# The high and low q row of a node side by side in the table, one window load per edge group: a graph network layer on one NeuronCore

## What is computed

```python
h  = maximum(layernorm(x), 0)
eq = h @ Wq + bq          # per node
ek = h @ Wk + bk          # per node
e  = edge_attr @ We + be  # per edge
m  = relu(eq[dst] + ek[src] + e)
ft = segment_sum(m, dst)
out = x + (ft @ Wr + br)
```

## Time and profile before

| | |
|---|---|
| median of 3 runs | 1135.48 us (1135.22 to 1139.48) |
| the profiled execution, device time | 1134.75 us |
| its span in the profile | 1132.9 us |
| mean granted clock of TensorE | 0.995 of full speed |
| PE, DVE, ACT, POOL busy | 96%, 83%, 76%, 75% of the span |
| HBM traffic | 272 GB/s over the span |

### The profile page before, as it was taken

The page is one execution under the profiler, slowest core; times in us unless marked ns, Lnnn a source line. Parts: engine busy times, 40 slices in busy tenths (PEclk is TensorE's granted clock), DMA queues, the critical chain, the costliest instruction groups (busy, mean ns, idle before and its releaser), DMA issues.

```text
span 1132.9 us, 28337 instructions
## 1 busy us (share of the span) xinstructions
PE 1091.0 (96%) x9166; PEld 1065.9 (94%) x9166; DVE 945.5 (83%) x1382; ACT 857.9 (76%) x1373; POOL 849.3 (75%) x949
## 2 busy tenths in 40 slices
PE   9979999999999999999999999999999999999998
PEld 8978999999999999999999999999999999998997
DVE  7778888888888888888888888888888888888887
ACT  7957877777777777787777777777777777777774
POOL 7877777777777777777777777777777777777773
PEclk9998999999999999999999999999999999999999
DMA  9789898999989988899998998889998899988882
GB/s 301 225 258 286 271 287 280 282 276 286 285 273 288 280 276 281 274 285 282 282 282 273 286 287 274 281 275 286 283 280 281 280 283 279 288 275 256 268 252 87
DMA packets 171122, 309.10 MB, mean 273 GB/s; under 512 B 30817, under 2 KB 117358, under 8 KB 171038
## 3 DMA queue, kind: packets, MB, share of 16 engines
q1 hardware_dynamic: 130590, 198.79, 53.3%
q0 software_dynamic: 39888, 108.97, 34.4%
q10 hardware_dynamic: 560, 0.52, 0.1%
HBM read 281.20 MB, written 26.95 MB: 272 GB/s over the span
## 4 chain that ended last, share of the span: by engine, by line
POOL 68%; issue 23%; PE 3%; DMA 2%; DVE 1%; ACT 1%; SPq 1%; POOLq 0%; ACTq 0%; DVEq 0%
POOL k_rows L727 67%; PE p_sum L1339 1%; PE p_edge L1339 1%; DMA hn<-in_x 1%; DMA k_table<-k_rows 0%; PE p_turn L1359 0%; DMA ft<-in_x 0%; POOL hn L651 0%; DVE stats L1008 0%; DVE p_edge L1182 0%; PE p_sum L1443 0%; SPq L489 0%; ACT k_rows L797 0%; POOL edge L665 0%; SPq L478 0%
## 5 line engine op out<-in xcount | busy, mean ns | idle before, releaser
L727 POOL DMA_INDIRECT k_rows<-k_table,src_idx x796 | 765.3, 961 | 246.3 <-issue 241.9
L1339 PE MATMUL p_edge<-we_hi,edge_hi 128*128 128x256 f32 x1662 | 473.7, 285 | 28.1 <-DVE m_lo L1191 22.3
L1339 PE MATMUL p_edge<-we_hi,edge_lo 128*128 128x256 f32 x1662 | 462.5, 278 | 0.0
L1339 PE MATMUL p_edge<-we_lo,edge_hi 128*128 128x256 f32 x1662 | 461.2, 277 | 0.0
L1182 DVE TENSOR_TENSOR p_edge<-p_edge,k_rows 128x1024 f32<-128x1024 f32 x208 | 256.0, 1231 | 162.4 <-DMA k_rows<-k_table,src_idx 133.8
L878 ACT ACTIVATE m_hi<-p_edge 128x1024 fp32r<-128x1024 f32 x208 | 213.8, 1028 | 205.3 <-DVE p_edge L1182 205.3
L1339 PEld LDWEIGHTS p_edge<-we_hi,edge_hi 128*128 128x128 f32 x1662 | 314.9, 189 | 48.9 <-issue 23.0
L1339 PEld LDWEIGHTS p_edge<-we_lo,edge_hi 128*128 128x128 f32 x1662 | 315.8, 190 | 0.0
L1339 PEld LDWEIGHTS p_edge<-we_hi,edge_lo 128*128 128x128 f32 x1662 | 313.5, 189 | 0.0
L1157 DVE TENSOR_TENSOR edge_lo<-edge,edge_hi 128x1024 fp32r<-128x1024 f32 x208 | 253.2, 1217 | 2.9 <-ACT edge_hi L822 2.9
L1191 DVE SCALAR_TENSOR_TENSOR m_lo<-p_edge,m_hi 128x1024 fp32r<-128x1024 f32 x208 | 252.6, 1215 | 0.5 <-ACT m_hi L878 0.5
(11 more groups left out here) (154 smaller groups left out, 1104.7 us busy)
## 6 DMA issues: line engine op xcount, KB each, us to landing
edge<-in_edges SPq DMA_DIRECT2D x208, 512.0 KB, 5.2
rel_row<-rel_table SPq DMA_DIRECT2D x208, 96.0 KB
q_win<-q_table SPq DMA_DIRECT2D x416, 48.0 KB
k_rows<-k_table,src_idx POOLq DMA_INDIRECT x796
q_table<-hn SPq DMA_DIRECT2D x46, 256.0 KB
pre<-in_x SPq DMA_DIRECT2D x55, 128.0 KB, 5.6
out_rows<-pre SPq DMA_DIRECT2D x55, 128.0 KB, 1.7
k_table<-k_rows SPq DMA_DIRECT2D x23, 256.0 KB, 4.8
```

Source lines behind the costliest of these rows:

```text
L727: nc.gpsimd.indirect_dma_start(out=k_rows[:, slot, j, :], out_offset=None, in_=k_table, in_offset=bass.IndirectOffsetOnAxis(ap=offsets, ax ...
L1339: ins = nc.tensor.matmul(target, a(h), b[:, h, :], start=(start and h == 0 and n == 0), stop=(stop and h == HALVES - 1 and n == 2))
```

## The change

A node's high and low q row lie side by side in `q_table`: row 2v is the high row of node v, row 2v + 1 its low row. A window of 48 nodes is then 96 rows in one piece, and `load_window` is one transfer of 96 rows in place of two of 48. Partition p of `q_win` now holds the row of node p // 2 of the window, so `lane_node` is computed anew: the parity of the partition number, halved, is taken from half the iota. This adds one integer instruction on DVE (`bitwise_and`) and one wait ahead of `lane_wrap`; `lane_node` takes a scalar_tensor_tensor in place of a tensor_tensor. Stores of q rows write 2 KB in one piece per partition where they wrote two of 1 KB. PE waits for 16 a group in place of 32.

```diff
-    q_table = nc.dram_tensor("q_table", (2, NODE_BLOCKS * LANES, D), F32R, kind="Internal").ap()
+    q_table = nc.dram_tensor("q_table", (2 * NODE_BLOCKS * LANES, D), F32R, kind="Internal").ap()
...
-    q_blocks = q_table.rearrange("s (b p) d -> s b p d", p=LANES)
+    q_blocks = q_table.rearrange("(b p s) d -> b p s d", p=LANES, s=2)
...
-        lane_id = sb("lane_id", [2 * WIN, 1], F32)
+        lane_id = sb("lane_id", [2 * WIN, 1], I32)
...
-        PREP_STEPS = SPAN_STEPS + 4 + CHUNKS + 2
+        PREP_STEPS = SPAN_STEPS + 5 + CHUNKS + 2
...
-                    sp.dma_start(q_blocks[:, b].rearrange("s p d -> p s d").bitcast(F32),
+                    sp.dma_start(q_blocks[b].bitcast(F32),
                                  q_parts[:, b].bitcast(F32)).then_inc(s_qfirst[v], 16)
...
                 after(sp, s_prod, n - 4)
-                for s in range(2):
-                    sp.dma_start(q_win[s * WIN:(s + 1) * WIN, slot, :].bitcast(F32),
-                                 q_table[s, bass.ds(w0, WIN), :].bitcast(F32)).then_inc(s_win[slot], 16)
+                sp.dma_start(q_win[0:2 * WIN, slot, :].bitcast(F32),
+                             q_table[bass.ds(w0 * 2, 2 * WIN), :].bitcast(F32)).then_inc(s_win[slot], 16)
...
-                if isinstance(it, int):
-                    target = q_blocks[:, it + FIRST_Q].rearrange("s p d -> p s d")
-                else:
-                    target = q_blocks[:, bass.ds(it + FIRST_Q, 1)].rearrange("s a p d -> (a p) s d")
+                target = q_blocks[it + FIRST_Q]
...
-            nc.gpsimd.iota(lane_raw[:], pattern=[[WIN, PASSES]], base=0, channel_multiplier=1,
+            nc.gpsimd.iota(lane_raw[:], pattern=[[2 * WIN, PASSES]], base=0, channel_multiplier=1,
...
+                nc.vector.tensor_scalar(lane_id[:], lane_id[:], 1, None, ALU.bitwise_and).then_inc(s_prep, 1)
...
-                nc.vector.tensor_scalar(lane_wrap[:], lane_id[:], float(WIN), float(WIN), ALU.is_ge, ALU.mult)\
-                    .then_inc(s_prep, 1)
+                dve.wait_ge(s_prep, SPAN_STEPS + 1)
+                nc.vector.tensor_scalar(lane_wrap[:], lane_id[:], 0.5, None, ALU.mult).then_inc(s_prep, 1)
...
-                dve.wait_ge(s_prep, SPAN_STEPS + 5)
+                dve.wait_ge(s_prep, SPAN_STEPS + 6)
...
-                nc.vector.tensor_tensor(lane_node[:], lane_raw[:], lane_wrap[:].to_broadcast([2 * WIN, PASSES]),
-                                        ALU.subtract).then_inc(s_prep, 1)
+                nc.vector.scalar_tensor_tensor(lane_node[:], lane_raw[:], 0.5, lane_wrap[:].to_broadcast([2 * WIN, PASSES]),
+                                               ALU.mult, ALU.subtract).then_inc(s_prep, 1)
...
-                pe.wait_ge(s_win[slot], 32 * (body + 1))
+                pe.wait_ge(s_win[slot], 16 * (body + 1))
```

## The result

| | before | after |
|---|---|---|
| median of 14 runs | 1134.72 us | 1141.18 us |
| lowest, highest | 1132.40, 1139.48 | 1139.34, 1146.09 |
| ratio, 95% interval | | 1.0058 (1.0047 to 1.0069) |
| span of the profiled execution | 1132.9 us | 1139.4 us |

The forecast was 1134.7 us, the range ended at 1138.0.

The account below looks back on a forecast made before the run. POOL was taken to bound the kernel, at 1.25 us a gather. The start's -0.8 us and DVE's +0.05 us made about -0.8 us against the median of 1135.48, so 1134.7 us; range 1131.0 to 1138.0.

Parts of the forecast that it names:

- What bounds the kernel: Whole loop: POOL's gathers set the pace, 0.947 + 0.30 = 1.25 us each, 1034 us of the 1132.9 us span.
- One q transfer for two, the loop: SP's window loads in the loop: 208 issues fewer, nothing waits on them; 0 taken, 0 to -1 us kept.
- becomes longer waiting at L489: SP's queue in the loop: about 0.5 us a group freed only lengthens SP's wait for PE to free the slot.
- The prediction's own sign of being wrong: Loop: among its signs, the 3.5 us of stretched gathers becoming 6 or more would show the prediction wrong.
- the gathers are not touched and not waited for: POOL's gathers of k rows in the loop: nothing changes for POOL, part of the term taken as 0.
- The start: Start of the kernel: SP issues the first loads 2.2 us earlier, POOL resumes sooner; -0.8 us, bounds 0 and 1.25 us.
- The added DVE step: DVE's preparation: the added `bitwise_and` on 96 x 1 costs +0.05 us, bounds 0.05 and 0.28 us.
- Faster, the catch-up goes too: Rival, after the start: PE has nothing to catch up, 7.3 us saved, 1128.2 us; chance 0.06.
- Slower, more gathers are stretched: Rival, loop: SP's earlier edge loads shift DVE, `edge_low` stretches gathers, 0.5 us a body, 1156 to 1157 us; chance 0.05.
- DVE's phase is set by `s_wrote`, not by loads: Loop: argument against the slower rival, that DVE's timing follows its wait for the gathers' descriptors; no size of its own.

Follow-up runs that it names:

- e9: The changed kernel with two register reads (0.9 us of pause) on SP behind the window load at u = 1 alone; 1133.27 us, ratio 0.9991 to before.
- e16: The kernel before with two reductions on DVE ahead of `edge_low` at u = 2 in the 50 unrolled bodies; 1158.33 us, ratio 1.0202.
- e10: The changed kernel with four register reads (1.8 us of pause) on SP behind the window load at u = 1; 1132.50 us, ratio 0.9984 to before.
- e11: The changed kernel with `load_next_x` moved from behind the window load at u = 2 to behind the one at u = 1; 1148.31 us, ratio 1.0126 to before.
- e12: The kernel before with one read of a window number into a register of DVE ahead of `edge_low` at u = 2; 1134.74 us, ratio 1.0002.

## Why the prediction was wrong

**What bounds the kernel**: right. POOL's step of 1.25 us sets the time before and after, and the lost microseconds are its own.

**One q transfer for two, the loop, "Off the path: 0"**: this is the step that failed. The term was worked out for the transfer itself, for the wait on it (right: PE waits for no window in the loop) and for DMA time (taken as 0 to -1 us; the queue has 9216 packets fewer, yet they took 53.1% of 16 x 1139.4 us where it was 53.3% of 16 x 1132.9, so no less). Of the 0.5 us by which SP's queue moves up it said that it "becomes longer waiting at L489". Part does, 0.31 us a group. But at u = 1 the next thing behind the window load is an edge load with nothing to wait for, and it moved up, from 13.5 to 12.9 or 13.3 us. The cost was the landing of other rows, those that POOL gathers: 5.15 us after the last gather in place of 4.88, and 5.1 us more of stretched gathers from 160 to 1000 us. The prediction's own sign of being wrong came true: the 3.5 us of stretched gathers in the loop became 7.5.

**"the gathers are not touched and not waited for"**: wrong in its second half. DVE waits for their landing, and at u = 2 it had 0.24 us to spare in the median, 0.12 of which is the delay from completion to start. The waits of before had the row:

```profile
DVE p_edge L1182 <- DMA k_rows<-k_table,src_idx: 133.8, 154, 1.9
```

I read it as the wait on `s_wrote` alone. At the other steps it nearly always is.

**The start**: -0.8 us forecast, about +1 us found. `load_next_x(0)` left at 77.23, 1.4 us earlier where I had 2.2: the window loads took SP 1.95 us less (4.10 for 6.05), but began 0.58 us later (72.15 for 71.57), as the four q stores ahead of them took 2.67 us in place of 2.07. But DVE's first add ran from 84.66, not 84.00, and PE's third product from 88.70, not 88.42. POOL's restart lies between 97.0 and 99.4 in the other profiles of this study without the totals following it (e9 has 99.37 and 0.9991), so I make nothing of 1 us there. What made it up is seen in part only: the eight gathers ahead of the restart began 0.67 us later (86.17, not 85.50), and one of them, at 89.92, took 1.99 us.

**The added DVE step**: `bitwise_and` took 0.12 us, as its neighbour did, and started 0.09 us after the one before it. Small, as said.

**Faster, the catch-up goes too**: did not happen; the stretch from 96 to 160 us is 6.2 us, 6.1 before.

**Slower, more gathers are stretched**: this is what happened, and it had a chance of 0.05. The mechanism and the price were right: 0.5 us a body, from `edge_low` running when a gather starts, and DVE made late by SP's earlier edge loads. It was put aside with "DVE's phase is set by `s_wrote`, not by loads", the same misreading. Its size was 14 more places and 5.1 us of stretch in the loop rather than 43 bodies, since the landing moved by 0.27 us across a threshold on which it already stood. The rule of the Trainium skill that the prediction cited for it, in "SBUF — State Buffer", section "Who interferes with whom", is borne out: `edge_low` has two SBUF inputs, the gather reads its indices, and e16 gives 0.82 us from the end of the one to the end of the other, while gathers that start beside `add_rows` (one SBUF input) took 0.96 us at the longest.

## What to carry to other kernels

An engine with time to spare can move the bound all the same: when a queue is made shorter, list what stands behind the removed instruction with nothing to wait for, and ask whose transfers are in flight when it starts. A wait that the profile puts down to a transfer has to be checked at each place in the loop, against the time of landing: the total over four steps hid the one with 0.1 us of slack. Where the pacing engine shares something with another, the other's phase is part of the bound, and a slip of half a microsecond costs as much as half a microsecond of the pacing engine.

## What the runs showed that I had not expected

- The landing of four gathers (512 KB), counted from the end of the last, took 5.15, 4.45 or 2.73 us, as one 512 KB load on the other queue was issued 1.8 us before, 0.7 us before or 0.4 us after that end (after, e9, e10).
- 128 KB of x ahead of that load (e11) cost more than was gained by the load leaving 0.6 us later: 1.0126, where it was 1.0058 without them.
- Register reads are a usable pause on SP (two of them move the next issue by 0.8 to 1.1 us) and no pause on DVE (e12).
- A 96-row transfer costs SP 0.343 us, two of 48 rows 0.84 us with what lies between.
